# Head 0's projections ahead of the FFN, token statistics in two halves, ternary masks on GpSimd, half-filled FFN blocks merged

## The chip, the core and the metric

One core of a Trainium2 chip. The metric is the device time of one execution in microseconds. TensorE (PE) multiplies matrices; VectorE (DVE), ScalarE (ACT) and GpSimd (POOL) work elementwise; SyncE (SP) only issues the DMAs.

## The reference

2048 tokens of width 256 pass a layernorm. The result xn goes into an attention of 16 heads (head width 128) and, beside it, into a gated feed-forward network (FFN) of width 704 whose weights are quantised to -1, 0 and 1:

```python
xn = _layernorm(x)
# attention
qkv = einsum('bsd,ed->bse', xn, Wqkv)          # 3 x 16 heads x 128
w = softmax(q k^T * 128 ** -0.5)
attn = einsum('bse,de->bsd', w v, Wout)
# ffn
def _quantize(w):
    gamma = mean(abs(w))
    return clip(round(w / (gamma + 1e-8)), -1, 1)
hidden = sigmoid(xn @ _quantize(w1).T) * (xn @ _quantize(w2).T)     # w1, w2: 704 x 256
ffn = hidden @ _quantize(w3).T                                      # w3: 256 x 704
out = x + attn + ffn
```

## The kernel before

Everything is kept in SBUF. Every operand of a matmul is split into a high part (rounded to the type that TensorE takes at full speed) and a low part (the rest): ScalarE copies the high part, VectorE or GpSimd subtracts it from the original. A product of two split operands is three matmuls (high-high, high-low, low-high). The quantised weights are exact, so the FFN needs two matmuls for each.

The tokens are worked on in 4 groups (G) of 512, each of 4 tiles (TG) of 128 tokens. Each engine has its own instruction list, written out by hand, and the engines are tied together by semaphores only.

Start. SP loads x in four transfers, then w1, w2, w3 (in two transfers, since 704 = 5 x 128 + 64), then head 0's Wk, Wq and Wv (`load_part`). VectorE takes the statistics of all 16 tiles (line 760), then the mean, the variance and, after ScalarE's root (line 578), a reciprocal and one Newton step; then it normalises group by group (`normalise`, line 789). TensorE transposes the normalised tiles into PSUM (`transpose_x`, line 392), ScalarE copies the high part (`xt_high`, line 600) and VectorE subtracts (`xt_low`, line 797). For the thresholds ScalarE sums the absolute weights (line 594), TensorE adds over the partitions with a matrix of ones (lines 424, 427) and VectorE makes half of gamma (lines 804 to 809). A weight is quantised as (w > gamma/2) - (w < -gamma/2), two VectorE instructions over the whole matrix: line 817 writes the mask `below`, line 820 does the rest.

FFN. Width 704 is cut into FB = 6 blocks; the last holds only FR = 64 rows, padded with zeros. For group g and block b, `ffn_up` makes x1 and x2 (2 x 4 matmuls of 512 columns into two PSUM banks), ScalarE the sigmoid (line 607), VectorE the product with x2 (`hidden`, line 838), ScalarE its high part (`hidden_high`, line 611) and GpSimd its low part (line 1022). `ffn_down` (lines 416, 418) then multiplies with w3: 8 matmuls of 256 columns for each block, into four halves of the banks ps_t and ps_o. VectorE adds the result to y (`add_ffn`, line 845). The transposes of groups 1 to 3 lie between the blocks of group 0, and w3 is quantised after its fourth product. Groups 1 to 3 are a hardware loop.

Then head 0's projections: `keys` (4 banks of 6 matmuls, line 333), `queries` (line 342, the first of four banks), `values` (line 352, three of four banks; the fourth comes in the head), with their high parts on ScalarE (lines 639, 643), the low parts on VectorE (lines 866, 871), and the values turned in blocks of 32 by VectorE (line 876) and moved by DMA. Then the heads: 16 times the same list of 16 query tiles, in which the projections of the next head lie between the products of this one. Each tile's logits (lines 362 to 364) wait for the exponentials of the tile before.

`part_low` (line 1009) is GpSimd's subtract for the head's weights.

Of the kernel before, what the change touches and what calls it, by code (L numbers as in the profile page):

```python
# [28 lines left out]
P = 128  # L29
# [9 lines left out]
FR = FF - (FB - 1) * P  # L39
G = 4  # L40
# [28 lines left out]
def build(nc, x_d, wqkv_d, wo_d, w1_d, w2_d, w3_d, out_d):  # L69
    ctx = ExitStack()  # L70
    with ctx:
# [10 lines left out]
        with ExitStack() as first:  # L82
            xn = sb("xn", [P, T, DIM], where=first)
            below = sb("below", [P, FB * DIM], where=first)
            junk = sb("junk", [P, FB * DIM], where=first)
# [3 lines left out]
        q_lo = sb("q_lo", [P, 2, 512], F32R)  # L89
        v_hi = sb("v_hi", [P, T, D], F32R)  # L90
        v_lo = sb("v_lo", [P, T, D], F32R)


        v_raw = sb("v_raw", [P, 4, T, BLK])
# [15 lines left out]
        with ExitStack() as early:  # L110
# [3 lines left out]
            w1_q = sb("w1_q", [P, C, FB * P], F32R, early)  # L114
            w2_q = sb("w2_q", [P, C, FB * P], F32R, early)
            w3_q = sb("w3_q", [P, FB, DIM], F32R, early)
# [12 lines left out]
            sig = sb("sig", [P, 2, CH], where=early)  # L129
            hid = sb("hid", [P, 2, CH], where=early)  # L130
            hid_hi = sb("hid_hi", [P, FB, CH], F32R, early)
            hid_lo = sb("hid_lo", [P, FB, CH], F32R, early)
# [4 lines left out]
        raw = sb("raw", [P, RAW_RING, 2, S])  # L137

# [17 lines left out]
        early_turned = [prob[:, E_RING - 1, j * 512:(j + 1) * 512] for j in range(3)]  # L156
# [30 lines left out]
        s_wq = sem("quantised_weights_ready")  # L187
        s_ln = sem("layernorm_step_done")
        s_std = sem("std_ready")
        s_xn = sem("normalised_ready")  # L190
        s_xtr = sem("normalised_transposed")
# [6 lines left out]
        s_hidl = sem("hidden_low_ready")  # L198
        s_down = sem("ffn_down_done")
# [41 lines left out]
        def _(sp):  # L241
            x_v = x_d.rearrange("(t p) c -> p t c", p=P)
            for g in range(G):
                sp.dma_start(y[:, g * TG:(g + 1) * TG, :], x_v[:, g * TG:(g + 1) * TG, :]).then_inc(s_x[g], 16)
            sp.dma_start(w1_raw[:], w1_d.rearrange("(c p) f -> p c f", p=P)).then_inc(s_w[0], 16)
            sp.dma_start(w2_raw[:], w2_d.rearrange("(c p) f -> p c f", p=P)).then_inc(s_w[1], 16)
            sp.dma_start(w3_raw[:, 0:FB - 1, :],
                         w3_d[0:(FB - 1) * P, :].rearrange("(b p) c -> p b c", p=P)).then_inc(s_w[2], 16)
            sp.dma_start(w3_raw[0:FR, FB - 1, :], w3_d[(FB - 1) * P:FF, :]).then_inc(s_w[2], 16)

# [13 lines left out]
            for part in (1, 0, 2):  # L264
                load_part(part, 0)
# [61 lines left out]
        def _(pe):  # L327
# [57 lines left out]
            def transpose_x(g):  # L385

                pe.wait_ge(s_xn, g + 1)
                for c in range(C):
                    if g:
                        pe.wait_ge(s_xtl, C * (g - 1) + c + 1)  # L390
                    for j in range(TG):
                        last = nc.tensor.transpose(ps_t[:, c, j * P:(j + 1) * P],
                                                   xn[:, g * TG + j, c * P:(c + 1) * P], ident[:])
# [17 lines left out]
            def ffn_down(g):  # L411
                for b in range(FB):
                    pe.wait_ge(s_hidl, g * FB + b + 1)
                    for j in range(TG):
                        dst = (ps_t if j < 2 else ps_o)[:, j % 2, 0:DIM]
                        nc.tensor.matmul(dst, hid_hi[:, b, j * P:(j + 1) * P], w3_q[:, b, :],
                                         start=(b == 0), stop=False)
                        last = nc.tensor.matmul(dst, hid_lo[:, b, j * P:(j + 1) * P], w3_q[:, b, :],
                                                start=False, stop=(b == FB - 1))
                last.then_inc(s_down, 1)  # L420

            pe.wait_ge(s_const, 1)
            pe.wait_ge(s_abs, 2)
            nc.tensor.matmul(ps_o[:, 0, 0:2], ones[:], abs_sum[:, 0:2], start=True, stop=True).then_inc(s_tot, 1)
            transpose_x(0)
            pe.wait_ge(s_abs, 3)
            nc.tensor.matmul(ps_o[:, 1, 0:1], ones[:], abs_sum[:, 2:3], start=True, stop=True).then_inc(s_tot, 1)

            pe.wait_ge(s_wq, 1)
            pe.wait_ge(s_xtl, C)  # L430
            for b in range(FB):
                ffn_up(0, b, b == 0)
                if b + 1 < G:
                    transpose_x(b + 1)
            pe.wait_ge(s_wq, 3)
            pe.wait_ge(s_xtl, C * G)
# [8 lines left out]
            pe.wait_ge(s_wsp[1], 1)  # L445
            for bank in range(4):
                keys(bank)
            pe.wait_ge(s_yacc, T)
            pe.wait_ge(s_wsp[0], 1)
            queries(ps_v[1], 0)  # L450
            pe.wait_ge(s_wsp[2], 1)
            values(ps_v[0], 0)
            pe.wait_ge(s_qlo, 1)
            values(ps_v[1], 1)
            pe.wait_ge(s_vt, 1)
            values(ps_v[0], 2)
# [16 lines left out]
            def head(h, first, final):  # L473
                for t in range(T):
# [28 lines left out]
                    if t == 0:  # L503
                        pe.wait_ge(s_vt, count(4, h, 2))
                        values(ps_v[1], 3)
# [70 lines left out]
        def _(act):  # L576
            act.wait_ge(s_ln, 4)
            nc.scalar.activation(std[:], var_eps[:], ACT.Sqrt).then_inc(s_std, 1)
# [18 lines left out]
            def xt_high(g):  # L597
                for c in range(C):
                    act.wait_ge(s_xtr, C * g + c + 1)
                    nc.scalar.copy(xt_hi[:, c, g * CH:(g + 1) * CH], ps_t[:, c, :]).then_inc(s_xth, 1)  # L600


            def sigmoid(g, b):
# [3 lines left out]
                nc.scalar.activation(sig[:, b % 2, :], ps_s[:, 2 * (b % 2), :], ACT.Sigmoid).then_inc(s_sig, 1)  # L607

            def hidden_high(g, b):
                act.wait_ge(s_hid, g * FB + b + 1)  # L610
                nc.scalar.copy(hid_hi[:, b, :], hid[:, b % 2, :]).then_inc(s_hidh, 1)
# [5 lines left out]
            xt_high(0)  # L617
# [3 lines left out]
            for part in (1, 0, 2):  # L621
                part_high(part, (0, 0), 0)
            for b in range(FB + 1):
                if b < FB:
                    sigmoid(0, b)
                if b + 1 < G:
                    xt_high(b + 1)
# [8 lines left out]

            def keys_high(h, bank):
                act.wait_ge(s_kproj, count(4, h, bank + 1))
                nc.scalar.copy(k_hi[:, bank * 512:(bank + 1) * 512], ps_s[:, bank, :]).then_inc(s_khi, 1)

            def queries_high(h, bank, src):
                act.wait_ge(s_qproj, count(4, h, bank + 1))
                nc.scalar.copy(q_hi[:, bank % 2, :], src).then_inc(s_qhi, 1)
# [41 lines left out]
            origin = (0, 0)  # L685
            for bank in range(4):
                keys_high(origin, bank)
            queries_high(origin, 0, ps_v[1])
# [66 lines left out]
        def _(dve):  # L755

            for t in range(T):
                if t % TG == 0:
                    dve.wait_ge(s_x[t // TG], 16)
                last = nc.vector.bn_stats(stats[:, t, :], y[:, t, :])  # L760
            last.then_inc(s_ln, 1)

            dve.wait_ge(s_ln, 1)
            nc.vector.tensor_tensor(mean[:], stats[:, :, 1], stats[:, :, 4], ALU.add)
            nc.vector.tensor_tensor(diff[:], stats[:, :, 1], stats[:, :, 4], ALU.subtract)
            nc.vector.tensor_tensor(var_eps[:], stats[:, :, 2], stats[:, :, 5], ALU.add).then_inc(s_ln, 1)
            dve.wait_ge(s_ln, 2)
            nc.vector.tensor_scalar(mean[:], mean[:], 0.5, None, ALU.mult)
            nc.vector.tensor_tensor(diff[:], diff[:], diff[:], ALU.mult)
            nc.vector.tensor_scalar(var_eps[:], var_eps[:], 1.0 / DIM, LN_EPS, ALU.mult, ALU.add).then_inc(s_ln, 1)  # L770
            dve.wait_ge(s_ln, 3)
            nc.vector.scalar_tensor_tensor(out=var_eps[:], in0=diff[:], scalar=0.25, in1=var_eps[:],
                                           op0=ALU.mult, op1=ALU.add).then_inc(s_ln, 1)
            dve.wait_ge(s_std, 1)
            nc.vector.reciprocal(rstd[:], std[:]).then_inc(s_ln, 1)

            dve.wait_ge(s_ln, 5)
            nc.vector.tensor_tensor(newton[:], rstd[:], rstd[:], ALU.mult).then_inc(s_ln, 1)
# [329 lines left out]
```

## Time and profile before

| | us |
|---|---|
| median of 3 runs | 1910.93 (1906.85 to 1912.75) |
| the profiled execution | 1910.57 |
| its span, first to last instruction | 1908.7 |
| TensorE busy | 1862.1 (98%) |
| VectorE busy | 1594.4 (84%) |
| GpSimd busy | 1347.9 (71%) |
| ScalarE busy | 1252.2 (66%) |

Times of rows are microseconds from the first instruction of the profiled execution, and durations in microseconds, unless they are marked as ns. The granted clock is the share of TensorE's full clock of 2.4 GHz that it was given over a stretch. A matmul's shown duration is longer than its share of the time when matmuls follow each other, since they overlap; how far their starts lie apart is what counts. "PEld" is the load of a matmul's weights, and "SPq" SyncE's queue, issuing.

### The profile page before, as it was taken

To read this page: it belongs to the slowest core of one execution; us is meant where nothing else is said; L and a number is where in the kernel's file an instruction comes from. 1 tells how busy PE (TensorE), PEld (TensorE's weight loads), DVE (VectorE), ACT (ScalarE), POOL (GpSimd) and SP (SyncE) were. 2 spreads that over 40 slices of the span, in tenths; PEclk is the share of its full clock that TensorE was granted. 3 is DMA by queue.
4 is the path that set the end of the run, shared out by engine and by line. 5 is a ranking of instruction groups with operands and counts; after the bars stand their busy time and mean duration, and the time that the engine had idled before them with its cause. 6 is when DMAs were issued, how large, how long until landed. Compare 5 with 4: busy or idle time off the path is not lost.

```text
span 1908.7 us, 33423 instructions
## 1 busy us (share of the span) xinstructions
PE 1862.1 (98%) x11588; PEld 1665.3 (87%) x11588; DVE 1594.4 (84%) x2088; ACT 1252.2 (66%) x1700; POOL 1347.9 (71%) x514
## 2 busy tenths in 40 slices
PE   5989999999999999999999999999999999999998
PEld 4868888898888989888888988888898988889887
DVE  6368888888888889888888988888898888888885
ACT  4337676666767666666767667676766667676665
POOL 2418687776868777686877768687776868776685
PEclk9999999999999999999999999999999999999999
DMA  3037677676767767676776767677676767767664
GB/s 106 0 74 177 160 168 170 153 175 156 175 159 170 172 153 172 160 173 156 175 171 154 171 160 172 158 175 171 154 171 160 169 161 171 175 147 171 156 159 128
DMA packets 195830, 298.65 MB, mean 156 GB/s; under 512 B 37888, under 2 KB 57024, under 8 KB 195776
## 3 DMA queue, kind: packets, MB, share of 16 engines
q1 hardware_dynamic: 195776, 298.01, 66.7%
q8 instruction: 24, 0.39, 0.1%
q14 instruction: 30, 0.25, 0.0%
HBM read 12.65 MB, written 2.10 MB: 8 GB/s over the span
## 4 chain that ended last, share of the span: by engine, by line
PE 79%; POOL 6%; SPq 5%; issue 4%; DVE 3%; ACT 1%; DMA 1%; POOLq 0%; DVEq 0%; ACTq 0%
PE ps_o L371 30%; PE ps_s L362 10%; PE ps_s L363 10%; PE ps_s L364 10%; SPq L279 5%; POOL parts L1035 4%; PE ps_t L352 4%; PE ps_s L333 4%; PE ps_t L342 4%; PE ps_s L405 2%; PE ps_o L380 1%; PE ps_o L382 1%; PE ps_o L381 1%; DVE prob L891 1%; DMA raw<-prob 1%
## 5 line engine op out<-in xcount | busy, mean ns | idle before, releaser
L1035 POOL TENSOR_TENSOR parts<-raw,parts 128x2048 fp32r<-128x2048 f32 x254 | 1175.7, 4629 | 443.6 <-ACT parts L669 443.5
L681 ACT ACTIVATE prob<-ps_s,neg_max 128x1024 f32<-128x1024 f32 x512 | 567.0, 1114 | 449.0 <-DVE neg_max L885 448.8
L881 DVE TENSOR_REDUCE row_max<-ps_s 128x1 f32<-128x1024 f32 x512 | 613.0, 1213 | 114.1 <-PE ps_s L364 95.7
L891 DVE STREAM_TRANSPOSE prob<-prob 128x1024 f32<-128x1024 f32 x508 | 599.5, 1218 | 60.7 <-ACT prob L681 60.3
L669 ACT CAST parts<-raw 128x2048 fp32r<-128x2048 f32 x254 | 486.3, 1915 | 105.8 <-DMA raw<-prob 104.3
L371 PE MATMUL ps_o<-parts,v_hi 128*128 128x256 f32 x4064 | 515.8, 280 | 4.8 <-POOL v_lo L1028 4.8
L371 PEld LDWEIGHTS ps_o<-parts,v_hi 128*128 128x128 f32 x4064 | 497.9, 189 | 20.5 <-POOL v_lo L1028 6.1
L362 PE MATMUL ps_s<-k_hi,q_hi 128*128 128x512 f32 x1024 | 402.6, 393 | 12.5 <-ACT prob L681 11.5
L363 PE MATMUL ps_s<-k_lo,q_hi 128*128 128x512 f32 x1024 | 400.3, 391 | 0.0
L364 PE MATMUL ps_s<-k_hi,q_lo 128*128 128x512 f32 x1024 | 400.1, 391 | 0.0
L371 PE MATMUL ps_o<-parts,v_lo 128*128 128x256 f32 x2032 | 275.6, 278 | 0.0
L371 PEld LDWEIGHTS ps_o<-parts,v_lo 128*128 128x128 f32 x2032 | 252.9, 188 | 0.0
L362 PEld LDWEIGHTS ps_s<-k_hi,q_hi 128*128 128x128 f32 x1024 | 192.8, 188 | 57.4 <-ACT prob L681 11.5
L364 PEld LDWEIGHTS ps_s<-k_hi,q_lo 128*128 128x128 f32 x1024 | 192.7, 188 | 41.0
L363 PEld LDWEIGHTS ps_s<-k_lo,q_hi 128*128 128x128 f32 x1024 | 192.8, 188 | 35.0
L911 DVE SCALAR_TENSOR_TENSOR y<-ps_o,inv_denom,y 128x256 f32<-128x256 f32 x256 | 111.1, 476 | 4.0 <-PE ps_o L382 4.0
L681 ACT ACTIVATION_READ_ACCUMULATOR prob<-ps_s,neg_max 128x1 f32 x512 | 98.6, 193 | 0.0
L342 PE MATMUL ps_t<-xt_hi,w_sp 128*128 128x512 f32 x256 | 89.5, 390 | 0.0
L352 PE MATMUL ps_t<-xt_hi,w_sp 128*128 128x512 f32 x256 | 89.2, 390 | 0.0
L333 PE MATMUL ps_s<-xt_hi,w_sp 128*128 128x512 f32 x256 | 81.5, 389 | 0.0
L895 DVE TENSOR_TENSOR o_lo<-ps_o,o_hi 128x256 fp32r<-128x256 f32 x127 | 53.9, 424 | 28.7 <-ACT o_hi L657 16.6
L1028 POOL TENSOR_TENSOR v_lo<-v_raw,v_hi 128x1024 fp32r<-128x1024 f32 x32 | 77.3, 2416 | 0.0
(111 smaller groups left out, 1571.6 us busy)
## 6 DMA issues: line engine op xcount, KB each, us to landing
raw<-prob SPq DMA_DIRECT2D x2032, 128.0 KB, 2.4
v_raw<-v_turned SPq DMA_DIRECT2D x244, 64.0 KB, 2.0
w_raw<-wqkv_dram SPq DMA_DIRECT2D x32, 128.0 KB, 2.5
y<-x_dram SPq DMA_DIRECT2D x4, 512.0 KB, 6.1
wo_raw<-wqkv_dram SPq DMA_DIRECT2D x16, 128.0 KB, 2.5
wo_raw<-wo_dram SPq DMA_DIRECT2D x16, 128.0 KB, 2.3
out_dram<-y SPq DMA_DIRECT2D x8, 256.0 KB, 2.7
w_raw<-w_dram SPq DMA_DIRECT2D x2, 704.0 KB, 10.6
```

What stands on the lines that cost most here:

```text
L333: last = nc.tensor.matmul(dst, w_sp[:, 1, c, w, :], x[:, c, bank * 512:(bank + 1) * 512], start=(n == 0), stop=(n == 3 * C - 1))
L342: last = nc.tensor.matmul(dst, w_sp[:, 0, c, w, :], x[:, c, col], start=(n == 0), stop=(n == 3 * C - 1))
L352: last = nc.tensor.matmul(dst, w_sp[:, 2, c, w, :], x[:, c, j * 512:(j + 1) * 512], start=(n == 0), stop=(n == 3 * C - 1))
L362: nc.tensor.matmul(ps_s[:, bank, :], q_hi[:, qb, tile], k_hi[:, col], start=True, stop=False)
L363: nc.tensor.matmul(ps_s[:, bank, :], q_hi[:, qb, tile], k_lo[:, col], start=False, stop=False)
L364: last = nc.tensor.matmul(ps_s[:, bank, :], q_lo[:, qb, tile], k_hi[:, col], start=False, stop=True)
L371: last = nc.tensor.matmul(ps_pv, v[:, kb, :], parts[:, kb, which].rearrange("p a q -> p (a q)"), start=(kb == 0 and v is v_hi and which == 1),
L669: nc.scalar.copy(half_of(1, half), moved(p, half)).then_inc(s_ph, 1)
L681: nc.scalar.activation(tile, logit, ACT.Exp, bias=neg_max[:, t:t + 1], scale=SCALE, accum_out=row_sum[:, t, half:half + 1]).then_inc(s_exp, 1)
L881: nc.vector.reduce_max(row_max[:, t, half:half + 1], ps_s[:, 2 * half:2 * half + 2, :].rearrange("p b n -> p (b n)"), AX_X).then_inc(s_mx, 1)
L891: nc.vector.transpose(tile, tile).then_inc(s_xp, 1)
L1035: nc.gpsimd.tensor_tensor(half_of(0, half), moved(p, half), half_of(1, half), ALU.subtract).then_inc(s_pl, 1)
```

## The change

1. SP loads x0, x1, Wk, Wq, x2, x3, Wv, and only then w1, w2 and w3.
2. The statistics and the layernorm's small operations are done for groups 0 and 1 and then for groups 2 and 3. GpSimd normalises group 3.
3. Head 0's keys, its first queries and three banks of its values are computed group by group between the transposes, ahead of the FFN. The groups' transposes use ps_t for group 0 and ps_o for the others.
4. GpSimd makes the masks of the quantised weights (`is_below`); VectorE does the other half. w3 is quantised after the third product of group 0.
5. The half-filled sixth block: the last 64 rows of w1 and of w2 share one block of 128 in `w1_q`, so one product of 4 matmuls makes both, x1 on partitions 0 to 63 and x2 on 64 to 127. The product's high part stays on partitions 64 to 127, its low part is written to 0 to 63 by VectorE, and w3's last 64 rows stand twice in `w3_q` (loaded again by a small DMA after the absolute sums), so that 4 matmuls do what 8 did.
6. Buffers are moved so that this fits: the early values have a tile of their own (`first_values`) instead of a row of `prob`, and `w3_q`, `hid_hi` and `hid_lo` are placed later.

```diff
-            for g in range(G):
+            load_x(0)
+            load_x(1)
+            load_part(1, 0)
+            load_part(0, 0)
+            load_x(2)
+            load_x(3)
+            load_part(2, 0)
...
+            sp.wait_ge(s_abs, 3)
+            sp.dma_start(w3_raw[FR:P, FB - 1, :], w3_d[FL:FF, :]).then_inc(s_w3_again, 16)
...  TensorE
-                for w, k in ((w1_q, 0), (w2_q, 1)):
+                for w, k in ((w1_q, 0), (w2_q, 1))[:1 if b == FB - 1 else 2]:
...
-                        last = nc.tensor.matmul(dst, hid_lo[:, b, j * P:(j + 1) * P], w3_q[:, b, :],
-                                                start=False, stop=(b == FB - 1))
+                        if b < FB - 1:
+                            nc.tensor.matmul(dst, hid_lo[:, b, j * P:(j + 1) * P], w3_q[:, b, :],
+                                             start=False, stop=False)
...
+            transpose_x(0)
+            transpose_x(1)
+            pe.wait_ge(s_xtl, C)
+            pe.wait_ge(s_wsp[1], 1)
+            keys(0)
+            pe.wait_ge(s_wsp[0], 1)
+            queries(ps_v[1], 0)
+            totals(2, slice(0, 2))
+            pe.wait_ge(s_wsp[2], 1)
+            values(ps_v[0], 0)
+            pe.wait_ge(s_xtl, 2 * C)
+            keys(1)
+            transpose_x(2)
+            pe.wait_ge(s_qlo, 1)
+            values(ps_v[1], 1)
+            pe.wait_ge(s_gamma, 3)
+            totals(3, slice(2, 3))
+            transpose_x(3)
+            keys(2)
+            pe.wait_ge(s_vt, 1)
+            values(ps_v[0], 2)
+            pe.wait_ge(s_xtl, 4 * C)
+            pe.wait_ge(s_gamma, 6)
+            keys(3)
             pe.wait_ge(s_wq, 1)
             for b in range(FB):
+                if b < 2:
+                    pe.wait_ge(s_klo, 2 * b + 2)
+                if b == FB - 1:
+                    pe.wait_ge(s_wshared, 1)
                 ffn_up(0, b, b == 0)
...  ScalarE
+            part_high(1, origin, 0)
+            part_high(0, origin, 0)
+            root(0)
+            part_high(2, origin, 0)
+            xt_high(0)
             act.wait_ge(s_w[0], 16)
             abs_sums(0, w1_raw)
+            xt_high(1)
             act.wait_ge(s_w[1], 16)
             abs_sums(1, w2_raw)
+            keys_high(origin, 0)
+            queries_high(origin, 0, ps_v[1])
+            root(1)
...
             abs_sums(2, w3_raw)
+            keys_high(origin, 1)
+            xt_high(2)
+            xt_high(3)
+            keys_high(origin, 2)
+            keys_high(origin, 3)
...  VectorE
+            statistics(0)
+            statistics(1)
+            layernorm(0)
             normalise(0)
+            normalise(1)
+            statistics(2)
+            xt_low(0)
+            xt_low(1)
+            statistics(3)
+            layernorm(1)
+            normalise(2)
+            keys_low(origin, 0)
+            queries_low(origin, 0, ps_v[1])
+            thresholds(1, ps_s[:, 3, 0:2], slice(0, 2))
+            values_turn(origin, 0, ps_v[0], early_turned[0])
+            xt_low(2)
+            keys_low(origin, 1)
+            values_turn(origin, 1, ps_v[1], early_turned[1])
+            thresholds(2, ps_s[:, 3, 2:3], slice(2, 3))
+            xt_low(3)
             quantise(0, w1_raw, w1_q[:, :, 0:FF])
+            keys_low(origin, 2)
+            quantise(1, w2_raw, w2_q[:], w1_q[:, :, FF:FB * P])
+            values_turn(origin, 2, ps_v[0], early_turned[2])
+            keys_low(origin, 3)
...
+                dve.wait_ge(s_hidh, g * FB + FB)
+                nc.vector.tensor_tensor(hid_hi[0:FR, FB - 1, :], hid[FR:P, (FB - 1) % 2, :], hid_hi[FR:P, FB - 1, :],
+                                        ALU.subtract).then_inc(s_hidlast, 1)
...  GpSimd
+            def is_below(i, raw):
+                pool.wait_ge(s_gamma, 3 if i < 2 else 6)
+                if i == 2:
+                    pool.wait_ge(s_wq, 1)
+                    pool.wait_ge(s_w3_again, 16)
+                nc.gpsimd.tensor_scalar(below_of(i, raw), raw[:], half_gamma[:, 1, i:i + 1], None, ALU.is_lt
+                                        ).then_inc(s_below, 1)
...
+            pool.wait_ge(s_ln, 16)
+            for t in range(3 * TG, T):
+                last = nc.gpsimd.tensor_scalar(xn[:, t, :], y[:, t, :], mean[:, t:t + 1], rstd[:, t:t + 1],
+                                               ALU.subtract, ALU.mult)
+            last.then_inc(s_xn_last, 1)
+            is_below(0, w1_raw)
+            is_below(1, w2_raw)
+            is_below(2, w3_raw)
```

In the first head TensorE waits, ahead of values(3), for the last addition of the FFN (`s_yacc`).

## Rows read from the trace of the kernel before

**Rows 1.** The page's busy time by engine.
```profile
PE 1862.1 (98%) x11588; PEld 1665.3 (87%) x11588; DVE 1594.4 (84%) x2088; ACT 1252.2 (66%) x1700; POOL 1347.9 (71%) x514
```
**Rows 2.** Stretches: length, busy time and count of each engine, granted clock, DMA.
```profile
31.10:50.50 19.40, 17.00 (x99) 15.02 (x98) 10.51 (x13) 8.19 (x15) 7.79 (x6) 0.91 0.00 1
83.90:100.60 16.70, 16.70 (x98) 14.61 (x98) 5.57 (x10) 6.75 (x12) 7.70 (x6) 1.00 0.00 1
```
**Rows 3.** Chain of waits, 0 to 110 us: start, length, what.
```profile
50.58 11.04 PE ps_s L405 x48
...
100.73 5.45 PE ps_s L333 x24
```
**Rows 4.** TensorE's timeline: first matmul of the keys, first of head 0's logits.
```profile
100.57 0.40 PE L333 MATMUL ps_s<-xt_hi,w_sp 128*128 128x512 f32 x1
...
111.82 0.39 PE L362 MATMUL ps_s<-k_hi,q_hi 128*128 128x512 f32 x1
```
**Rows 5.** Timeline of the start: start us, length, what, idle before.
```profile
0.74 2.09 SPq L244 DMA_DIRECT2D y<-x_dram  x4
...
4.42 2.91 DVE L760 BATCH_NORM_STATS2 stats<-y 128x6 f32<-128x256 f32 x8 [4.42 <-DMA y<-x_dram]
...
13.33 0.22 ACT L578 ACTIVATE std<-var_eps 128x16 f32<-128x16 f32 x1 [11.32 <-DVE var_eps L772]
13.45 1.36 ACT L594 ACTIVATE junk<-w_raw 128x1408 f32<-128x1408 f32 x1
...
14.71 1.38 DVE L789 TENSOR_SCALAR xn<-y,mean,rstd 128x256 f32<-128x256 f32 x4
...
22.00 1.28 ACT L607 ACT_TABLE_LOAD   x1
```
**Rows 6.** DMA issues of x1 and x3: KB, us from issue to landing.
```profile
y<-x_dram SPq DMA_DIRECT2D x1, 512.0 KB, 4.7
...
y<-x_dram SPq DMA_DIRECT2D x1, 512.0 KB, 8.6
```
**Rows 7.** Groups by line and shape, two windows: xcount, busy us, mean ns.
```profile
L866 DVE TENSOR_TENSOR k_lo<-ps_s,k_hi 128x512 fp32r<-128x512 f32 x4 | 2.8, 692 | 2.5 <-ACT k_hi L639 2.5
L1022 POOL TENSOR_TENSOR hid_lo<-hid,hid_hi 128x512 fp32r<-128x512 f32 x24 | 30.9, 1297 | 42.2 <-ACT hid_hi L611 42.2
...
L999 POOL MEMSET w_raw<- 64x256 f32 x1 | 0.3, 310 | 0.1
L1001 POOL MEMSET ones<- 128x128 f32 x1 | 0.2, 205 | 0.1
```
**Rows 8.** Timeline: VectorE's two-part quantising, and GpSimd beside it.
```profile
17.68 0.95 DVE L817 TENSOR_SCALAR below<-w_raw,half_gamma 128x1408 f32<-128x1408 f32 x1
...
18.66 1.69 DVE L820 SCALAR_TENSOR_TENSOR w_q<-w_raw,half_gamma,below 128x1408 fp32r<-128x1408 f32 x1
...
21.45 0.73 POOL L1009 TENSOR_TENSOR w_sp<-wo_raw,w_sp 128x256 fp32r<-128x256 f32 x1 [19.07 <-ACT w_sp L583]
21.46 1.47 DVE L817 TENSOR_SCALAR below<-w_raw,half_gamma 128x1408 f32<-128x1408 f32 x1
...
22.96 2.03 DVE L820 SCALAR_TENSOR_TENSOR w_q<-w_raw,half_gamma,below 128x1408 fp32r<-128x1408 f32 x1
...
24.92 3.07 DVE L789 TENSOR_SCALAR xn<-y,mean,rstd 128x256 f32<-128x256 f32 x8
...
40.00 1.41 POOL L1022 TENSOR_TENSOR hid_lo<-hid,hid_hi 128x512 fp32r<-128x512 f32 x1 [0.54 <-ACT hid_hi L611]
...
40.31 2.71 DVE L820 SCALAR_TENSOR_TENSOR w_q<-w_raw,half_gamma,below 128x1536 fp32r<-128x1536 f32 x1
```
**Rows 9.** TensorE's timeline at 22 us: two up matmuls that follow each other.
```profile
22.26 0.63 PE L405 MATMUL ps_s<-xt_lo,w_q 128*128 128x512 f32 x1
...
22.69 0.63 PE L405 MATMUL ps_s<-xt_hi,w_q 128*128 128x512 f32 x1
```
**Rows 10.** The stretch behind group 0's stall, columns as in rows 2.
```profile
43.08:47.50 4.42, 4.42 (x24) 4.42 (x25) 1.14 (x2) 1.22 (x2) 2.51 (x2) 0.62 0.02 4
```

More of the change, by code:

```diff
@@ L80, in build @@
         xt_lo = sb("xt_lo", [P, C, S], F32R)
[L82 to L85, printed above, removed]
         k_hi = sb("k_hi", [P, S], F32R)
@@ L89, in build @@
         q_lo = sb("q_lo", [P, 2, 512], F32R)
+        with ExitStack() as first:
+            xn = sb("xn", [P, T, DIM], where=first)
         v_hi = sb("v_hi", [P, T, D], F32R)
         v_lo = sb("v_lo", [P, T, D], F32R)
+        with ExitStack() as first:
+            junk = sb("junk", [P, FB * DIM], where=first)
         v_raw = sb("v_raw", [P, 4, T, BLK])
@@ L154, in half_of, with below_of, turned_x @@
             return parts[:, half * KH:(half + 1) * KH, which].rearrange("p b a q -> p a b q")
-        early_turned = [prob[:, E_RING - 1, j * 512:(j + 1) * 512] for j in range(3)]
+        early_turned = [first_values[:, j * 512:(j + 1) * 512] for j in range(3)]
+        def below_of(i, raw):
+            return below[:, i % 2, 0:raw.shape[1] * raw.shape[2]].rearrange("p (b c) -> p b c", b=raw.shape[1])
+        def turned_x(g):
+            return ps_o if g else ps_t
         ps_v = (ps_t[:, 0, :], ps_t[:, 1, :])
@@ L444, in _ @@
             pe.wait_ge(s_hid, G * FB)
[L445 to L456, printed above, removed]
             def product_step(h, p, half, first=False):
@@ L503, in head @@
                     if t == 0:
+                        if first:
+                            pe.wait_ge(s_yacc, T)
                         pe.wait_ge(s_vt, count(4, h, 2))
@@ L755, in _ @@
         def _(dve):
[L757 to L766, printed above, removed]
@@ L841, in add_ffn @@
-            def add_ffn(g):
-                dve.wait_ge(s_down, g + 1)
-                for j in range(TG):
-                    tile = y[:, bass.ds(g * TG + j, 1), :].rearrange("p t c -> p (t c)")
-                    nc.vector.tensor_tensor(tile, (ps_t if j < 2 else ps_o)[:, j % 2, 0:DIM], tile,
-                                            ALU.add).then_inc(s_yacc, 1)
-            for b in range(FB):
-                hidden(0, b)
-                if b + 1 < G:
-                    xt_low(b + 1)
-                if b == 0:
-                    normalise(G - 1)
-                if b == 3:
-                    dve.wait_ge(s_gamma, 6)
-                    quantise(2, w3_raw, w3_q[:])
@@ L857, in _, with quantise @@
-            add_ffn(0)
-            with dve.Fori(1, G) as g:
-                for b in range(FB):
-                    hidden(g, b)
-                add_ffn(g)
+            def quantise(i, raw, q, shared=None):
+                dve.wait_ge(s_below, i + 1)
+                is_below = below_of(i, raw)
+                n = raw.shape[2] if shared is None else FL
+                nc.vector.scalar_tensor_tensor(out=q, in0=raw[:, :, 0:n], scalar=half_gamma[:, 0, i:i + 1],
+                                               in1=is_below[:, :, 0:n], op0=ALU.is_gt, op1=ALU.subtract
+                                               ).then_inc(s_wq, 1)
+                if shared is not None:
+                    nc.vector.scalar_tensor_tensor(out=shared, in0=raw[:, :, FL:FF],
+                                                   scalar=half_gamma[:, 0, i:i + 1], in1=is_below[:, :, FL:FF],
+                                                   op0=ALU.is_gt, op1=ALU.subtract).then_inc(s_wshared, 1)
@@ new lines, in hidden, with add_ffn @@
+            def hidden(g, b):
+                dve.wait_ge(s_sig, g * FB + b + 1)
+                if b >= 2:
+                    dve.wait_ge(s_hidl, g * (FB - 1) + b - 1)
+                n, bank = (FR, 2 * (b % 2)) if b == FB - 1 else (P, 2 * (b % 2) + 1)
+                nc.vector.tensor_tensor(hid[P - n:P, b % 2, :], ps_s[P - n:P, bank, :], sig[P - n:P, b % 2, :],
+                                        ALU.mult).then_inc(s_hid, 1)
+            def add_ffn(g):
+                dve.wait_ge(s_hidh, g * FB + FB)
+                nc.vector.tensor_tensor(hid_hi[0:FR, FB - 1, :], hid[FR:P, (FB - 1) % 2, :], hid_hi[FR:P, FB - 1, :],
+                                        ALU.subtract).then_inc(s_hidlast, 1)
+                dve.wait_ge(s_down, g + 1)
+                for j in range(TG):
+                    tile = y[:, bass.ds(g * TG + j, 1), :].rearrange("p t c -> p (t c)")
+                    nc.vector.tensor_tensor(tile, (ps_t if j < 2 else ps_o)[:, j % 2, 0:DIM], tile,
+                                            ALU.add).then_inc(s_yacc, 1)
@@ L878, in maximum @@
+            for b in range(FB):
+                hidden(0, b)
+                if b == 2:
+                    quantise(2, w3_raw, w3_q[:])
+            add_ffn(0)
+            with dve.Fori(1, G) as g:
+                for b in range(FB):
+                    hidden(g, b)
+                add_ffn(g)
             def maximum(h, t):
```

194 lines of the change are left out of this document (93 added, 101 removed).

## The prediction

> **What bounds the kernel now.** The page's busy shares come first: TensorE is busy for 98% of the span [rows 1], so in the heads only less TensorE work or fewer gaps can save time. The change touches only what stands ahead of head 0, so I cut that into stages. Group 0 of the FFN ends at 50.5 us, with TensorE idle for 2.4 of the last 19.4; a later group takes 16.7 us, with TensorE never idle [rows 2]. The chain of waits says that a group is 48 up matmuls in 11.04 us (0.23 us each), so its 48 down matmuls take 16.7 - 11.04 = 5.66 us (0.118 each), and that the keys' 24 matmuls take 5.45 us (0.227 each) [rows 3]. From the end of the FFN to head 0's first logits TensorE does only head 0's projections, 100.57 to 111.82: 11.25 us [rows 4]. So from 50.5 us on the matmuls set the end, and before it, where TensorE waits for others, whatever is late: the tokens, VectorE's queue, the weights' masks. Those stages have to be replayed; the later ones only counted.
>
> **What leaves the path.** (a) 48 projection matmuls (24 keys, 6 queries, 18 values; values(3) stays in the head) move ahead of the FFN: -11.2 us behind it. The ACT table load for the exponential, 1.28 us a load [rows 5], then lies under the last down matmuls, as it lay under the value matmuls before. (b) The merged sixth block takes 4 up matmuls for 8 and 4 down matmuls for 8: 4 x 0.23 + 4 x 0.118 = 1.39 us a group, so -4.2 us over groups 1 to 3; group 0's share is in its own working below. The new end of a group is sigmoid, product, copy, and then a VectorE subtract in place of GpSimd's 1.30: about 4 x 0.7 = 2.8 us. The 40 down matmuls ahead of the last four take 4.7 us and cover it; without that cover it would cost up to 2.8. GpSimd has one of these subtracts fewer, so buffers come free no later.
>
> **What group 0 costs now.** I replay VectorE's queue as it is now written out. Stats of tokens 0 and 1 end at 7.33 (8 in 2.91 us from 4.42) [rows 5]. The root now stands on ACT behind two casts that wait for Wk and Wq. Their DMAs stand behind x0 and x1; x1 landed 4.7 us after its issue, the fourth x 8.6 [rows 6], and the four issues took 2.09 us [rows 5]. So Wq lands between 6.6 and 9.5; I take 7.8. Cast 0.4 and the root's table load 1.28, which can't go ahead of the casts: root at 9.4, where the statistics alone would give 8.3. From root to normalise 1.38 [rows 5], so normalise(0), (1) run 10.8 to 13.5 (1.38 each). x2 and x3 come later than before, behind two more transfers of 128 KB, but even the slowest x of before was in by 10.9 and x2's stats are not due before 13.5: hidden. stats(2) to 15.0, xt_low(0) and (1) to 18.5 (the second waits for ACT, which has Wv's cast and an absolute sum of 1.36 [rows 5] between its copies), stats(3) 20.0, layernorm(1) 2.4 (its root waits behind ACT's copies of keys(0) and queries(0), which suffices if TensorE, busy from 12.3 on, is at the upper clock by 16.5; otherwise +1.3): 22.4. normalise(2) 24.1; low halves of keys(0) and queries(0), 0.69 each and a little less back to back [rows 7], 25.4; thresholds(1) 25.9; values turned 26.6; xt_low(2) 27.9; keys(1) 28.6; values turned 29.3; thresholds(2) 29.8; xt_low(3) 31.1.
>
> Then the masks, on GpSimd since 25.9. The trace has no such GpSimd operation. From below: memset, 0.205 for 128 elements and 0.310 for 256, 0.83 ns an element, 1.3 us for 1408. From above: the two-input subtract, 0.73 for 256 and 1.30 for 512 [rows 7, 8], 2.2 ns, 3.3 us. With one input it lies between; I take 2.2 us. Masks 0 and 1 then end at 28.1 and 30.3 and quantise(0), 1.69 alone, runs 31.1 to 32.8. GpSimd takes mask 2 (2.4 us, to 35.2) at once, VectorE keys(2) to 33.5, and then quantise(1) comes upon mask 2. What that does the trace shows: alone the quantise step took 1.69 and the compare 0.95. Beside a GpSimd subtract the compare (21.46) took 1.47, the next quantise 2.03, and the third, begun at 40.31 behind a subtract that ran from 40.00 to 41.41, took 2.71 and so ended 1.6 after that subtract: its time for 1536 elements alone [rows 8]. One waits for the other. So quantise(1) begins at 35.2: 36.7, 37.0 with the shared block, values turned 37.7, keys(3) 38.4. The second bank pair is free only then, and up(0,1) starts. By contrast eight normalise steps beside a subtract took 3.07 where 8 x 0.345 are 2.8 [rows 8]; I charged 0.3 for normalise(2) beside GpSimd's normalise(3).
>
> The Trainium skill ("SBUF — State Buffer", Who interferes with whom) has the same rule, an exclusive lock held for the whole instruction; by that rule, the trace agrees, the wait of 1.7 us for mask 2 stands. It speaks against putting masks on GpSimd. The Trainium skill's "GPSIMD Engine Reference" (4.1 Engine selection) calls one-input work roughly line rate; that would be an estimated 1.2 us a mask, the wait would shrink to 0.6 and the sum be about 1 us lower.
>
> Clock: matmuls of 512 columns start 0.43 us apart at 22.3 us [rows 9], the lower level (1.2 GHz), and 0.23 apart later. After the 2.4 us idle ahead of 43.08 the granted clock was 0.62 over the next 4.4 us [rows 10]. TensorE now has little to do from 33 to 36.8, so I put the first matmuls of group 0 at the lower level: up(0,1) 38.4 to 41.0, of which 0.8 for the clock. Blocks 2, 3, 4 to 46.6. After product(0,2), 44.4, w3 is quantised for 1.8 (free) to 2.7 (as before): 46.7, product(0,3) 47.4, up(0,5) to 48.3, a stall of 0.8. 44 down matmuls: 53.5. So group 0 ends 3.0 us later than before: +3.0.
>
> Sum against the profiled execution, 1910.57 us (span 1908.7, 1.9 around it): -11.2 - 4.2 + 3.0 = -12.4, 1898.2. The profiled execution lies 0.4 below the median of the runs, so it serves for both. A shift of 0.3%, 5.7 us, is about what a measurement of this kernel can tell from none. Other edits at nothing: w3's last rows loaded again (64 KB, wanted after 33 us; SP waits for the third absolute sum, by 24 us, and behind it stand Wout's load and head 1's weights, wanted in head 0); the first values' moves, which now lie in the FFN; two memsets fewer; values(3) waiting for the last FFN add, which is done 1.7 us after the FFN while the first logits take 2.7. If that cover were gone it would cost 1.
>
> **Rivals.** (A) The lock and the slow clock cost more: masks at 3.3 us each hold quantise(0) to 32.5 (+1.4) and mask 2 holds quantise(1) another 1.2; TensorE is at the lower level in the first projections (+1.3) and in up(0,1) and (0,2) (+1.6 more). Together 5.5: 1904. For it, the rows of blocked steps; against, that TensorE is busy without a gap from 12.3. (B) The front is quicker: Wq in by 6.6 (-1.1), masks at memset's rate, 1.3 (quantise(1) then waits until 34.2, -1.0), no fall of the clock (-0.8), no stall for w3 (-0.8): 1894.5. (C) Logits come earlier but head 0 doesn't pass it on, because something tied to absolute time is late there. Head 0 starts with waits for maxima and exponentials that move along with it, and I find no transfer in it that the change doesn't bring forward; only the 4.2 of the merge would stay: 1906. (D) Slower: the comparison with a pointer operand is no simple operation for GpSimd. Masks 0 and 1 stand one behind the other from 25.9; VectorE wants the second by 33.5. The gain of 12.4 is gone when mask 1 ends 12.4 later than 35.2, my hold for mask 2: at 47.6, so 10.9 us a mask, 7.7 ns an element, 3.5 times the two-input rate. At 14 us a mask: 1917. Nothing in the trace is as slow.
>
> **How the numbers follow.** Forecast 0.66, own range 1895 to 1902; A 0.16; B 0.10; C 0.06; D 0.02. Likeliest 1898. B's 1894.5 less one us of the spread of the runs is the lower end, 1893; A's 1904 is the upper. Faster by over 0.3% (below 1905.2): nearly all of the forecast, A and B, 0.90; within it C and a corner of A, 0.08; slower D, 0.02.
>
> **What would show it.** After: 88 matmuls and about 15.3 us for each of groups 1 to 3; first logits near 99.4 us, directly behind down matmuls; head 0 from there on as long as before. Group 0 ends near 53.5. GpSimd's masks near 2.2 us; quantise(1) longer than 1.7 beside mask 2. The root behind a table load behind Wq's cast. Wrong if the root waits for Wq beyond 10 us, if group 0 ends outside 50 to 58, or if head 0 lengthens.

## The result and the profile after

The changed kernel takes 1903.11 us (median of 5 runs, 1899.86 to 1904.45) where the kernel before takes 1910.93: a ratio of 0.9958, 95% interval 0.9948 to 0.9969. That is 7.8 us, clear of the 0.3% that a measurement of this kernel can tell. It lies inside the stated bounds of 1893 to 1904, but outside the forecast's own 1895 to 1902 and 5.1 us above its likeliest value: it came out where rival A was. The profiled execution took 1899.86 us, its span 1898.0; it is the fastest of the five.

Head 0's first logits say where the time went without the scatter of the heads behind them. The timeline of TensorE in the changed kernel:

```profile
103.94 0.40 PE L389 MATMUL ps_s<-k_hi,q_hi 128*128 128x512 f32 x1
```

They start at 103.94, before at 111.82 [rows 4]: 7.88 us, the whole gain of the median. (The two profiled executions differ by 10.7; the other 2.8 lie in the heads, within their scatter.) From there to the end of the span it is 1794.1 us, before 1796.9; over all the kernels below it lies between 1794.1 and 1797.0. Head 0 itself, from its first logits to the copy of head 1's first keys, takes 106.86 us here and 107.07 before (106.8 to 107.3 in all): it passes the gain on. So the first logits serve as the measure, above all for the five kernels that were run once (e1, e3, e7, e8 and e9).

The stages (columns as in rows 2; a stretch is as long as it was asked for), in the chain of waits one group's up matmuls, and the first matmuls of groups 1, 2 and 3; the last line is the first matmul of group 1 in the kernel before:

```profile
57.57:72.90 15.33, 15.33 (x89) 13.35 (x88) 6.27 (x11) 6.97 (x12) 6.45 (x5) 1.00 0.01 2
36.36:39.73 3.37, 0.00 (x1) 0.01 (x1) 3.37 (x2) 0.00 (x0) 2.84 (x1) 0.57 0.02 5
39.73:43.30 3.57, 3.57 (x8) 2.82 (x9) 2.10 (x4) 0.60 (x1) 0.00 (x0) 0.50 0.22 53
```
```profile
73.26 10.13 PE ps_s L435 x44
```
```profile
57.57 0.40 PE L435 MATMUL ps_s<-xt_hi,w_q 128*128 x1
...
73.09 0.40 PE L435 MATMUL ps_s<-xt_hi,w_q 128*128 x1
...
88.50 0.40 PE L435 MATMUL ps_s<-xt_hi,w_q 128*128 x1
```
```profile
50.42 0.39 PE L405 MATMUL ps_s<-xt_hi,w_q 128*128 x1
```

From first matmul to first matmul a group takes 15.4 to 15.5 us where it took 16.7 [rows 2]: 44 up matmuls in 10.13, where there were 48 in 11.04 [rows 3]. (The stretch of 15.33 above ends 0.2 us before group 2 begins.) But group 0 ends at 57.57, where the matmuls of group 1 begin; before, at 50.42. The three terms are -11.25 (projections), -3.8 (groups 1 to 3: 46.37 for 50.15, from 50.42 to 100.57) and +7.15 (group 0): -7.9. The forecast had -11.2, -4.2 and +3.0. The third is the one to look into. Its timeline, all engines:

```profile
6.68 0.40 ACT L633 CAST w_sp<-w_raw 128x256 fp32r<-128x256 f32 x1
7.11 1.28 ACT L628 ACT_TABLE_LOAD   x1
8.79 0.21 ACT L628 ACTIVATE std<-var_eps 128x8 f32<-128x8 f32 x1 [0.40 <-DVE var_eps L835]
...
21.32 1.61 DVE L851 TENSOR_SCALAR xn<-y,mean,rstd 128x256 f32<-128x256 f32 x4
21.39 5.03 POOL L1097 TENSOR_SCALAR xn<-y,mean,rstd 128x256 f32<-128x256 f32 x4 [10.00 <-DVE rstd L846]
...
26.41 7.66 POOL L1090 TENSOR_SCALAR below<-w_raw,half_gamma 128x1408 f32<-128x1408 f32 x2
...
27.86 1.29 DVE L859 TENSOR_TENSOR xt_lo<-ps_o,xt_hi 128x512 fp32r<-128x512 f32 x2
...
30.29 4.59 DVE L878 SCALAR_TENSOR_TENSOR w_q<-w_raw,half_gamma,below 128x1408 fp32r<-128x1408 f32 x1 [1.14 <-POOL below L1090]
...
35.05 4.16 POOL L1090 TENSOR_SCALAR below<-w_raw,half_gamma 128x1536 f32<-128x1536 f32 x1 [0.98 <-issue]
35.41 4.26 DVE L878 SCALAR_TENSOR_TENSOR w_q<-w_raw,half_gamma,below 128x1280 fp32r<-128x1280 f32 x1
```
```profile
39.73 0.80 PE L435 MATMUL ps_s<-xt_hi,w_q 128*128 128x512 f32 x1 [3.59 <-DVE w_q L878]
...
40.49 0.65 DVE L889 TENSOR_TENSOR k_lo<-ps_s,k_hi 128x512 fp32r<-128x512 f32 x1
...
47.63 1.30 POOL L1107 TENSOR_TENSOR hid_lo<-hid,hid_hi 128x512 fp32r<-128x512 f32 x1 [0.54 <-ACT hid_hi L664]
47.81 2.73 DVE L878 SCALAR_TENSOR_TENSOR w_q<-w_raw,half_gamma,below 128x1536 fp32r<-128x1536 f32 x1
...
49.46 2.21 POOL L1107 TENSOR_TENSOR hid_lo<-hid,hid_hi 128x512 fp32r<-128x512 f32 x1 [0.54 <-ACT hid_hi L664]
...
51.28 0.47 PE L435 MATMUL ps_s<-xt_hi,w_q 128*128 128x512 f32 x1 [1.20 <-DVE hid L933]
```

Read it against the replay in the prediction. Up to xt_low(3) VectorE is early. The root is at 8.79 (forecast 9.4). Wq's cast (6.68) and the table load were over by 8.39, and the root waited the last 0.40 us for VectorE's variance: the transfer of Wq, which the forecast took as the limit, was none. xt_low(3) ends at 29.15 (31.1). From there it is late. Two masks of 1408 elements take GpSimd 7.66 us, 3.8 each and not 2.2, and they begin only at 26.41 because GpSimd's four normalise steps took 5.03. Quantise(0) begins with the first mask's end, at 30.29, and lasts 4.59 us, until 0.8 us after the second mask; quantise(1) 4.26, until 0.46 after the third. TensorE starts w2's half of the first product after 3.59 us of idleness (its idle time before 39.73), at a granted clock of 0.50 for the next 3.6 us (a stretch of 3.57 us above: 1.2 GHz, 8 matmuls). Before 51.28 it stands for 1.20 more, since the fourth product waits for w3's quantise step of 2.73, which in turn ended 1.6 us after the GpSimd subtract that it met.

### The profile page after: what moved, and what is told of

It reads as the page before. It is cut to its first block, busy times and chain, and to the rows that moved or that the text cites. A ratio compares the mean times of both kernels' runs of the same rounds, so it can differ in the third digit from the quotient of the medians.

```text
span 1898.0 us, 33380 instructions
## 1 busy us (share of the span) xinstructions
PE 1855.2 (98%) x11556; PEld 1659.1 (87%) x11556; DVE 1599.3 (84%) x2098; ACT 1254.7 (66%) x1702; POOL 1358.2 (72%) x515
## 4 chain that ended last, share of the span: by engine, by line
PE 79%; POOL 6%; SPq 5%; issue 4%; DVE 3%; DMA 1%; ACT 1%; POOLq 0%; DVEq 0%; ACTq 0%
PE ps_o L398 31%; PE ps_s L389 10%; PE ps_s L390 10%; PE ps_s L391 10%; SPq L306 4%; POOL parts L1120 4%; PE ps_t L379 4%; PE ps_t L369 4%; PE ps_s L360 3%; PE ps_s L435 2%; PE ps_o L407 1%; PE ps_o L409 1%; PE ps_o L408 1%; DVE prob L969 1%; DMA raw<-prob 1%
## 5 line engine op out<-in xcount | busy, mean ns | idle before, releaser
L389 PE MATMUL ps_s<-k_hi,q_hi 128*128 128x512 f32 x1024 | 403.2, 394 | 11.2 <-ACT prob L744 10.3
```

Of the source, the lines that this page charges most:

```text
L389: nc.tensor.matmul(ps_s[:, bank, :], q_hi[:, qb, tile], k_hi[:, col], start=True, stop=False)
```

## The experiments

Each is an edit to the changed kernel unless it says otherwise. First logits in brackets are at 111.82 before and at 103.94 in the changed kernel. The kernel before was measured again beside them: 1909.84 beside e1 to e4, 1910.35 beside e5 to e7, and once, 1910.15, beside e8 and e9.

**e1: the third mask later (100.46).** Here GpSimd's mask of w3 waits for the quantise step of w2.

```diff
-                    pool.wait_ge(s_wq, 1)
+                    pool.wait_ge(s_wq, 2)
```


> Only edit to the changed kernel: GpSimd's mask of w3 waits until w2 is quantised, not w1. In the changed kernel quantise(1) took 4.26 us, from 35.41, beside that mask (35.05 to 39.21). Theory (VectorE's quantise step and GpSimd's mask hold each other up): quantise(1) falls to about 1.5, its time for 1280 elements by the 1.69 for 1408 before; keys(3)'s low half ends 2.7 us earlier, TensorE's 3.6 us idle ahead of up(0,1) shrinks by as much, and the first logits come at 103.94 - 2.7 = 101.2 us. Rival (the quantise step is slower in this kernel by itself, its operands now in other buffers): it stays near 4.3 and the logits near 103.9.

```profile
30.36 4.60 DVE L878 SCALAR_TENSOR_TENSOR w_q<-w_raw,half_gamma,below 128x1408 fp32r<-128x1408 f32 x1 [1.15 <-POOL below L1090]
...
35.48 1.53 DVE L878 SCALAR_TENSOR_TENSOR w_q<-w_raw,half_gamma,below 128x1280 fp32r<-128x1280 f32 x1
```

Quantise(1), at 35.48, took 1.53 us in place of 4.26, with the same operands; quantise(0), still beside the second mask, took 4.60. The first logits came 3.5 us earlier, 0.8 more than expected. The trace shows where: TensorE's slow stretch began already at 35.35 here, in w1's half of the first product, and was over at 38.94, so that of the matmuls from w2's half on four were slow and not eight. The rival falls.

**e9: all masks in turn (102.72).** The second mask waits for the first quantise step as well, the third as in e1.

```diff
+                if i == 1:
+                    pool.wait_ge(s_wq, 1)
                 if i == 2:
-                    pool.wait_ge(s_wq, 1)
+                    pool.wait_ge(s_wq, 2)
```


> The changed kernel with GpSimd's second and third mask each waiting for the quantise step before it, so that no quantise step runs beside a mask. Theory (a quantise step of 1.7 us takes 4.6 only because a mask runs beside it): quantise(0) takes 1.7, from 30.3 to 32.0; the second mask 32.0 to 35.8; quantise(1) 1.5, to 37.4, where e1 (third mask alone moved) had 37.0; first logits between 100 and 101.5. Rival (the step is slow because it reads what GpSimd has just written): 4.6 us again, quantise(1) past 41, logits past 105.

```profile
30.36 1.68 DVE L878 SCALAR_TENSOR_TENSOR w_q<-w_raw,half_gamma,below 128x1408 fp32r<-128x1408 f32 x1 [1.14 <-POOL below L1092]
31.96 0.68 DVE L889 TENSOR_TENSOR k_lo<-ps_s,k_hi 128x512 fp32r<-128x512 f32 x1
36.09 1.55 DVE L878 SCALAR_TENSOR_TENSOR w_q<-w_raw,half_gamma,below 128x1280 fp32r<-128x1280 f32 x1 [3.44 <-POOL below L1092]
```
```profile
26.48 3.84 POOL L1092 TENSOR_SCALAR below<-w_raw,half_gamma 128x1408 f32<-128x1408 f32 x1
32.22 3.83 POOL L1092 TENSOR_SCALAR below<-w_raw,half_gamma 128x1408 f32<-128x1408 f32 x1 [1.90 <-DVE w_q L878]
```
```profile
37.69 0.79 PE L435 MATMUL ps_s<-xt_hi,w_q 128*128 128x512 f32 x1 [4.39 <-DVE w_q L878]
```

Both quantise steps take what they take alone, 1.68 and 1.55. The masks take 3.84 and 3.83, as long as beside a quantise step: in these meetings, where the mask began first, GpSimd lost nothing and VectorE all of it. The range was missed by 1.2 us: quantise(1) now waits 3.44 us for the mask, and TensorE, idle for 4.39, starts at the lower level, twelve matmuls of it (37.69 to 42.98). Against e1, which differs only in the second mask, e9 is 2.3 us later, 0.6 by quantise(1)'s end and most of the rest by the clock. So making the second mask wait costs more than its meeting with quantise(0) does. The third mask's wait in e1 is free, since nobody waits for that mask.

**e3 and e8: why a mask takes 3.8 us (105.06 and 103.55).** e3 gives the masks a constant threshold, e8 a multiplication in their place.

```diff
-                nc.gpsimd.tensor_scalar(below_of(i, raw), raw[:], half_gamma[:, 1, i:i + 1], None, ALU.is_lt
+                nc.gpsimd.tensor_scalar(below_of(i, raw), raw[:], -0.399, None, ALU.is_lt     # e3
+                nc.gpsimd.tensor_scalar(below_of(i, raw), raw[:], 0.001, None, ALU.mult       # e8
```


> Changed kernel with a constant, -0.399, as the threshold of GpSimd's three masks in place of the measured one (this alters which weights near the threshold become -1). It asks why a mask took 3.83 us, 2.7 ns an element, where GpSimd's two-input subtract takes 2.2 ns. Theory 1 (the threshold read from memory as a pointer makes the compare slow): about 2.2 us or less a mask, quantise(0) ends about 3 us earlier. Theory 2 (a compare is as slow on GpSimd with either operand): 3.8 us, nothing moves.

> The changed kernel with GpSimd's three masks replaced by one-input multiplications with a constant, of the same shape (the weights' -1 are lost: the quantised weights become 0, 1 and fractions near it). With a constant threshold a mask took 3.76 us (7.51 for two), with a measured one 3.83. Theory 1 (every such one-input instruction costs GpSimd about 2.7 ns an element, whatever its operation): 3.8 us again. Theory 2 (a comparison is dear): about 3.1 us or less, which is the two-input subtract's 2.2 ns for 1408 elements.

Groups by line and shape of GpSimd, changed kernel, then e3's timeline, then e8's groups:

```profile
L1090 POOL TENSOR_SCALAR below<-w_raw,half_gamma 128x1408 f32<-128x1408 f32 x2 | 7.7, 3842 | 0.0
L1097 POOL TENSOR_SCALAR xn<-y,mean,rstd 128x256 f32<-128x256 f32 x4 | 5.0, 1266 | 10.0 <-DVE rstd L846 10.0
L1090 POOL TENSOR_SCALAR below<-w_raw,half_gamma 128x1536 f32<-128x1536 f32 x1 | 4.2, 4156 | 1.0 <-issue 1.0
```
```profile
26.84 7.51 POOL L1090 TENSOR_SCALAR below<-w_raw 128x1408 f32<-128x1408 f32 x2
```
```profile
L1090 POOL TENSOR_SCALAR below<-w_raw 128x1408 f32<-128x1408 f32 x2 | 7.5, 3768 | 0.0
```

Neither the pointer nor the comparison is dear: 3.84, 3.76 and 3.77 us. From 1408 to 1536 elements it grows by 0.31 us, 2.5 ns an element with about 0.4 us around them. GpSimd's one-input instruction is slower than its two-input subtract, which took 1.30 for 512 [rows 7] and 2.42 for 1024 in the heads. Why, no run shows: the type and the layout of the operands weren't varied. A normalise step with two operations and two pointers takes 1.27 us for 256 elements, VectorE 0.35. The first logits of the two lie 1.1 above and 0.4 below the changed kernel though the masks are alike; the clock differs: from 44 to 46 us e3 was granted 0.62, e8 and the changed kernel 1.00.

**e4: the merge alone, on the kernel before (105.96; ratio 0.9962, 0.9948 to 0.9975).** All edits of item 5 of the change, nothing else; its quantising stays on VectorE.

```diff
-                for w, k in ((w1_q, 0), (w2_q, 1)):
+                for w, k in ((w1_q, 0), (w2_q, 1))[:1 if b == FB - 1 else 2]:
...
+                nc.vector.tensor_tensor(hid_hi[0:FR, FB - 1, :], hid[FR:P, (FB - 1) % 2, :], hid_hi[FR:P, FB - 1, :],
+                                        ALU.subtract).then_inc(s_hidlast, 1)
```


> The kernel before with the merged sixth block alone: 88 matmuls a group for 96, everything else in its old place. Theory (the merge gives its share of matmul time in every group, and its new subtract is covered by the other down matmuls): a group takes 15.3 us for 16.7, first logits 4 x 1.39 = 5.6 us earlier, at 106.3, the median near 1905.4 (ratio 0.997). Rival (the last block's longer way over ScalarE and VectorE becomes the end of each group): less than 2 us gained.

```profile
105.96 0.39 PE L368 MATMUL ps_s<-k_hi,q_hi 128*128 128x512 f32 x1
```

5.86 us earlier, for 5.6 expected, and not quite in the expected places: 1.9 in group 0 (1.39 expected) and 4.0 in groups 1 to 3 (4.2). By the median it gained 7.2 us on its own measurement of the kernel before, where the whole change gained 7.8: most of what the change brought is this part. All the rest, with 11.25 us of matmuls moved ahead, brought 2.0 us more at the first logits.

**e2: the masks of w1 and w2 back on VectorE (99.24; ratio 0.9923, 0.9909 to 0.9937).**

```diff
             def quantise(i, raw, q, shared=None):
+                if i < 2:
+                    mask(i, raw)      # VectorE: below_of(i, raw) = raw < -gamma / 2
...
-                    pool.wait_ge(s_wq, 1)
+                    pool.wait_ge(s_wq, 2)
...
-            is_below(0, w1_raw)
-            is_below(1, w2_raw)
             is_below(2, w3_raw)       # waits for the quantise step of w2
```


> Changed kernel with the masks of w1 and w2 back on VectorE, directly ahead of their quantise steps; w3's mask stays on GpSimd and waits until w2 is quantised. Theory (GpSimd's masks of 3.8 us and the blocking make the front late): VectorE's queue has 2 x 0.95 more, but quantise(0) ends at 29.2 + 0.95 + 1.69 = 31.8 in place of 34.9, quantise(1) at about 35.2 in place of 39.7; group 0 of the FFN ends 4.5 us earlier, first logits near 99.4, the median near 1898.6 (ratio to before 0.9935). Rival (the late end of group 0 comes from the clock and the order, not from the masks): first logits within 1 us of 103.9 and no change against the changed kernel.

```profile
28.98 0.94 DVE L876 TENSOR_SCALAR below<-w_raw,half_gamma 128x1408 f32<-128x1408 f32 x1
29.95 1.68 DVE L885 SCALAR_TENSOR_TENSOR w_q<-w_raw,half_gamma,below 128x1408 fp32r<-128x1408 f32 x1
...
32.16 0.94 DVE L876 TENSOR_SCALAR below<-w_raw,half_gamma 128x1408 f32<-128x1408 f32 x1
33.14 1.55 DVE L885 SCALAR_TENSOR_TENSOR w_q<-w_raw,half_gamma,below 128x1280 fp32r<-128x1280 f32 x1
```
```profile
34.74 0.51 PE L435 MATMUL ps_s<-xt_hi,w_q 128*128 128x512 f32 x1 [1.84 <-DVE w_q L885]
...
36.20 0.79 PE L435 MATMUL ps_s<-xt_hi,w_q 128*128 128x512 f32 x1 [0.25 <-DVE k_lo L896]
36.80 0.63 PE L435 MATMUL ps_s<-xt_lo,w_q 128*128 128x512 f32 x1
37.22 0.63 PE L435 MATMUL ps_s<-xt_hi,w_q 128*128 128x512 f32 x1
```

4.7 us earlier for 4.5 expected, and in the median 14.2 us below the kernel before (1895.62 for 1909.84). The rival falls. A mask costs VectorE 0.94 us.

**e5, e6, e7: what is left in group 0.** All on top of e2.

```diff
-                if b == 2:
+                if b == 0:                       # e5; e6: b == 1
                     quantise(2, w3_raw, w3_q[:])
...  e6, TensorE, between wait and first product of group 0
+                if b == 0:
+                    repeat_first()               # w1's product of block 0, thrown away
+                    repeat_first()
...  e7, VectorE
             normalise(2)
+            normalise(3)
...  e7, GpSimd
-            for t in range(3 * TG, T):
-                last = nc.gpsimd.tensor_scalar(xn[:, t, :], y[:, t, :], mean[:, t:t + 1], rstd[:, t:t + 1],
-                                               ALU.subtract, ALU.mult)
```


> e2_masks01_vector with w3 quantised after the first product of group 0, not the third. In e2 VectorE stood idle for 3.1 us between the first and the second product (37.3 to 40.4), GpSimd's mask was done at 39.01, and TensorE stood for 1.2 us at 46.4 because the fourth product waited for w3's quantise step (2.72 us beside a subtract). Theory (that stall is the third term of the late group 0): the stall goes, w3's step takes 1.6 to 1.9 in the gap, first logits at 99.24 - 1.2 = 98.0, ratio to before about 0.992. Rival (the stall only moves, since the step now begins at 39.0 and holds the second product): first logits at 99.2.

> e2_masks01_vector with w3 quantised after the second product, and w1's first product of group 0 made three times, the first two thrown away (8 matmuls more, 1.84 us at the upper clock), which fills TensorE's idle 1.84 us ahead of w2's. In e2 TensorE was idle for 1.84 us at 32.9 and 0.25 at 35.9, and then at the lower clock from 36.2 to 39.3: 8 matmuls in 3.4 us, not 1.84. Theory (the idle time brings the lower clock, and that holds group 0): with the gap filled, up(0,1) takes 1.84 us and the first logits come 1.2 (the w3 stall) + 1.3 earlier, near 96.8; ratio about 0.991. Rival (VectorE's products are what group 0 waits for, whatever TensorE's clock): no earlier than e5_w3_early.

> e2_masks01_vector with the last group normalised by VectorE as well (4 x 0.35 us) and not by GpSimd (5.03 us for four, beside which VectorE's own four took 1.61 and not 1.38). Theory 1 (GpSimd's slow normalise is hidden and spares VectorE's queue 1.38): w2's quantise step ends 1.1 us later and the first logits come at 100.4. Theory 2 (GpSimd delays the transposes of group 3 more than it spares): first logits at 99.2 or earlier.

Timelines of TensorE: e5 at its last block of group 0, then e6, then e7.

```profile
41.76 0.51 PE L435 MATMUL ps_s<-xt_hi,w_q 128*128 128x512 f32 x1 [0.15 <-DVE hid L940]
```
```profile
36.48 0.50 PE L435 MATMUL ps_s<-xt_hi,w_q 128*128 128x512 f32 x1 [0.28 <-DVE k_lo L904]
36.81 0.39 PE L435 MATMUL ps_s<-xt_lo,w_q 128*128 128x512 f32 x1
37.04 0.40 PE L435 MATMUL ps_s<-xt_hi,w_q 128*128 128x512 f32 x1
...
43.38 0.50 PE L435 MATMUL ps_s<-xt_hi,w_q 128*128 128x512 f32 x1 [1.13 <-DVE hid L948]
```
```profile
35.88 0.50 PE L432 MATMUL ps_s<-xt_hi,w_q 128*128 128x512 f32 x1 [1.85 <-DVE w_q L882]
...
37.35 0.51 PE L432 MATMUL ps_s<-xt_hi,w_q 128*128 128x512 f32 x1 [0.28 <-DVE k_lo L893]
37.69 0.40 PE L432 MATMUL ps_s<-xt_lo,w_q 128*128 128x512 f32 x1
```

e5 (98.23; ratio 0.9929, 0.9915 to 0.9942): the stall of 1.20 us is gone, but for 0.15, and the first logits come 1.0 earlier for 1.2 expected. e6 (97.91; 0.9934, 0.9920 to 0.9949): with the gap filled the matmuls after it start 0.33 and then 0.23 us apart, where in e2 they started 0.60 and 0.42 apart, so up(0,1) is at the upper level. That part of the theory holds; the expected 96.8 was missed because w3's quantise step, after the second product, lay beside a subtract of GpSimd again (2.86 us) and the stall of 1.13 us at 43.38 stayed. e6 is still 0.3 us ahead of e5, against its rival, but only in one execution of each. e7 (98.99) doesn't decide between its theories by the end, but the parts add up. In VectorE's queue quantise(1) ended 1.1 us later, as theory 1 has it. But TensorE, idle for 1.85 us as in e2 (1.84), went on at the upper level (0.34 and 0.23 apart), which e2 did not: up(0,1)'s eight matmuls took 1.96 us and not 3.36. Later by 1.15 and quicker by 1.4 is the 0.25 that e7 lies ahead. So theory 1 holds for the queue, and the clock behind a pause of this length came out either way, worth 1.4 us in one execution. Each first-logits time here is one execution's and carries this uncertainty: differences of a microsecond between kernels rest on the steps shown, not on the totals. In the medians e2, e5 and e6 can't be told apart: 1895.62, 1896.24, 1895.64.

## Why the prediction came out as it did

The direction, the path and two of the three terms were right; the third was too small by 4 us, which put the result outside the forecast's own range. **Projections ahead:** -11.25 for -11.2. Nothing behind them is tied to absolute time (rival C): head 0's waits moved along. **Merge:** 15.46 us a group for 15.3, and over groups 1 to 3 -3.8 for -4.2: the 88 matmuls that are left lie 0.9% further apart than in the kernel before, and why is not shown; e4 has the whole of it, -5.86 for -5.6 with group 0's share. The new subtract is covered: nothing in a later group waits for it. **Group 0:** it ended at 57.57 for 53.5, +7.15 for +3.0, and here the step that failed is the mask's price. The prediction put a GpSimd mask at 2.2 us with 3.3, the two-input rate, as the upper bound. It measured 3.84, above the bound: the trace of before has for GpSimd only memsets, one small select and two-input subtracts, and the assumption that one input is no dearer than two was not in any row. GpSimd's four normalise steps had no price in the prediction. They took 5.03 us, so the masks began at 26.41 and not at 25.9, though their threshold was there at 24.6. The low halves of keys(3) were therefore ready at 41.14 and not 38.4, although the front ran 2.0 us ahead of the replay. That is 2.7 of the missing 4.1 us. The rest is in about equal parts the clock (w2's half of the first product was at the lower level too, so up(0,1) began at 41.60 and not at 41.14) and the stall for w3, 1.2 for 0.8, with a slower start behind it.

The meeting of mask and quantise step was foreseen for w2; it took place for w1 as well, since the masks were long and the replay had VectorE reach that step only after both. Together with the third mask's early start the masks of w1 and w2 cost 4.7 us (e2 against the changed kernel), of which e1 gives back 3.5 by moving a wait. That is rival A's mechanism: A had 5.5 us more than the forecast, 1904, and measured were 1903.1. The forecast and A shared the mechanism and differed in the mask's price and the clock. That A's sum fits is in part luck: its price of a mask, 3.3, was still too low, and its slow clock in the first projections (1.3 us) didn't come, since the granted clock was 1.00 from 12.3 to 16.5.

The Trainium skill's page "SBUF — State Buffer" (Who interferes with whom) has the loser fully blocked for the whole instruction. The meetings here agree that one loses, and that it is the later one. They do not agree on fully: quantise(0), 1.68 alone, ended 0.8 us after the mask, and quantise(1), 1.53 alone, 0.46 us after it, so by these spans a part of each step had been done beside the mask. Where the other side is a GpSimd subtract the trace agrees nearly: w3's step ended 1.6 us after the subtract (47.63 + 1.30) and takes 1.82 alone (e5), and it then held up GpSimd in turn, whose next subtract (49.46) took 2.21 for 1.30 and ended 1.13 after the step. The Trainium skill's "GPSIMD Engine Reference" (4.1 Engine selection) calls one-input work roughly line rate, and by that the sum would have been 1 us lower; the 2.7 ns an element measured here decides against it.

## What to carry to other kernels

An engine that is idle is no free place for work: ask what the instruction costs there, from a row of the same form and not of a similar one, and whether it holds up the engine that waits for the result. Where two engines hold each other up like this, letting the work that nobody waits for start later (one number, 3.5 us) can give back most of it; where the result is wanted, waiting cost more (e9 against e1). And moving work ahead of a stage pays only as far as the front has room on the engine that is late there: of 11.25 us moved, 2.0 arrived with the masks on GpSimd, and 6.7 with two of them on VectorE.

## What the hardware showed beyond what was expected

GpSimd's one-input instruction with float operands took 3.84 us for 1408 elements and 4.16 for 1536, the same with pointer or constant and for comparison and multiplication; its two-input subtract of 1024 takes 2.42. A meeting lengthens the instruction that begins second: VectorE's quantise step behind a mask took 4.59 for 1.69, while the mask took 3.84 with and without; GpSimd's subtract behind w3's quantise step took 2.21 for 1.30. TensorE's clock after a pause of 1.84 us fell in e2, four matmuls and 0.25 us of idleness later, and stayed up after 1.85 us in e7. In the changed kernel the four matmuls behind a pause of 3.16 us (34.94) still ran at the upper level, 0.33 and 0.23 apart; after 3.59 us, and in e9 after 4.39 us, it was at the lower one.
